# A gated cross-attention and FFN kernel: FFN weights prepared in attention's last iterations, and a new placing of work over the slots of a batch

## The reference

```python
x = x + tanh(g_xattn[0]) * xattn(layernorm(x), ctx, ctx, Wq, bq, Wk, bk, Wv, bv, Wo, bo)
x = x + tanh(g_ffn[0])   * ffn(layernorm(x), w_gate, w_up, w_down)
# xattn: 32 batches, 256 positions, width 256, 16 heads of 16, rotary q and k,
#        keys within 50 positions of the query only, softmax, output projection
# ffn:   every weight is rounded in blocks of 32 to 4 bits and scaled back (lpbq_dequant);
def lpbq_dequant(w):
    wb = w.reshape(O, I // 32, 32)
    s = maximum(max(abs(wb), -1) / 7, 1e-12)
    return (clip(round(wb / s), -8, 7) * s).reshape(O, I)
#        activations are rounded to 16 bits by the largest absolute value of the whole tensor
#        (after x, up, gate, silu(gate), silu(gate) * up), inner width 768
```

## Time and profile before

| | us |
|---|---|
| median of 3 runs | 1405.16 (1403.41 to 1405.55) |
| the profiled execution | 1403.11 |
| its span in the trace | 1401.4 |
| `prepare`, to DVE's first instruction of attention | 48.3 |
| attention, from there to DVE's first instruction of the FFN | 48.3 to 843.0 |
| FFN | 843.0 to the end |

### The profile page before, as it was taken

How to read it: one execution, slowest core, us unless ns; L and a number is a source line. 1 busy time by engine, 2 the same in 40 slices (tenths; PEclk the granted TensorE clock), 3 DMA queues, 4 the chain that set the end, 5 groups by cost and what they waited for, 6 DMA issues and landing times. The chain is left out here.

```text
span 1401.4 us, 27833 instructions
## 1 busy us (share of the span) xinstructions
PE 1209.1 (86%) x8960; PEld 796.4 (57%) x8992; DVE 1214.9 (87%) x3602; ACT 832.9 (59%) x1336; POOL 562.6 (40%) x1360
## 2 busy tenths in 40 slices
PE   3367989898989898998989858999899979977998
PEld 2245666666666666666767643444333334436887
DVE  4678998998998999999999836998899989997986
ACT  2225665666675666667565545664677779983332
POOL 1127777776777777778777640000000000000000
PEclk7679999999999999999999988999999999998999
DMA  3175767666666667675756311222455455556764
GB/s 113 30 166 124 165 140 156 141 156 147 149 149 147 151 146 160 147 160 142 179 128 156 89 35 56 101 103 100 157 186 189 165 180 198 187 177 203 235 237 165
DMA packets 132369, 207.27 MB, mean 148 GB/s; under 512 B 11159, under 2 KB 97050, under 8 KB 126106
## 3 DMA queue, kind: packets, MB, share of 16 engines
q1 hardware_dynamic: 132250, 205.86, 54.0%
HBM read 125.60 MB, written 79.69 MB: 146 GB/s over the span
## 5 line engine op out<-in xcount | busy, mean ns | idle before, releaser
L586 ACT ACTIVATE probs<-psum 128x356 f32<-128x356 f32 x512 | 210.2, 464 | 235.2 <-PE psum L851 235.0
L697 DVE CUSTOM_DVE_ANT_0 psum<-psum,band 128x178 f32<-128x178 f32 x1024 | 318.2, 372 | 18.5 <-PE psum L834 13.0
L519 POOL TENSOR_SCALAR_AFFINE_SELECT probs<-probs 128x154 f32<-128x154 f32 (+1 forms) x512 | 222.9, 444 | 168.0 <-ACT probs L586 163.3
L1013 PE MATMUL psum<-xnT,w_upT 128*128 (+1 forms) x1152 | 260.9, 384 | 19.1 <-DVE maxima L1237 8.8
L1013 PEld LDWEIGHTS psum<-xnT,w_upT 128*128 128x128 f16 x1152 | 109.8, 99 | 170.1 <-issue 32.4
L834 PE MATMUL psum<-k_stack,q_stack 96*128 96x178 bf16 x1024 | 145.7, 246 | 56.2 <-DVE smax L697 50.9
L528 POOL TENSOR_SCALAR_AFFINE_SELECT probs<-probs 128x254 f32<-128x254 f32 (+1 forms) x512 | 189.7, 394 | 0.0
L851 PE MATMUL psum<-q_stack,k_stack 98*128 98x178 bf16 x1024 | 129.5, 242 | 16.1 <-DMA q_stack<-shiftT 9.2
L834 PEld LDWEIGHTS psum<-k_stack,q_stack 96*128 96x128 bf16 x1024 | 75.1, 99 | 119.0 <-DVE smax L697 101.9
L697 DVE DVE_READ_ACCUMULATOR2_ANT smax<- 128x1 f32 x1024 | 142.6, 139 | 0.0
L1613 PE MATMUL psum<-w_downT,xnT 128*128 128x256 f16 x1152 | 128.1, 275 | 16.0 <-DVE xnT L1563 16.0
(11 more groups left out here) (189 smaller groups left out, 2271.1 us busy)
## 6 DMA issues: line engine op xcount, KB each, us to landing
k_parts_scratch<-k_parts SPq DMA_DIRECT2D x32, 384.0 KB, 2.6
q_parts_scratch<-q_parts SPq DMA_DIRECT2D x32, 384.0 KB, 2.6
k_stack<-k_parts_scratch SPq DMA_DIRECT2D x32, 384.0 KB, 5.1
q_stack<-q_parts_scratch SPq DMA_DIRECT2D x32, 384.0 KB, 7.4
gate_scratch<-g_stage SPq DMA_DIRECT2D x16, 768.0 KB, 3.3
g_in<-gate_scratch SPq DMA_DIRECT2D x16, 768.0 KB, 4.6
sig_scratch<-w_gateT SPq DMA_DIRECT2D x32, 384.0 KB, 2.3
sig_again<-sig_scratch SPq DMA_DIRECT2D x32, 384.0 KB, 3.4
```

Of the source, the lines that this page charges most:

```text
L519: nc.gpsimd.affine_select(out=t[:, :, 0:n], in_=t[:, :, 0:n], pattern=[[0, 2], [1, n]], compare_op=ALU.is_ge, fill=0.0, base=WINDOW - off, ...
L586: nc.scalar.activation(ring_tile(probs, b, pair, c)[:].rearrange("p e j -> p (e j)"), scoreT_bank[c][:, 0:2 * SPAN], ACT.Exp, scale=DK ** ...
L697: ins = nc.vector.tensor_tensor_reduce(out=mine, in0=mine, in1=keep["band"][:, t, :], scale=1.0, scalar=-3e38, op0=ALU.add, op1=ALU.max, a ...
L1013: last = nc.tensor.matmul(bank[:], weights[wp][:, c * I + f * P:c * I + (f + 1) * P], x_parts[:, c, bass.ds(j * (2 * TILE) + xp * TILE, TI ...
```

## The change

`prepare` no longer loads or prepares the FFN weights, and has no `partition_all_reduce`. It loads c and x of batch 0 first, then the attention weights in the order Wo, Wk, Wq, Wv, and makes the output bias right after Wo.

The FFN weights are loaded by SP at the beginning of iteration 33 into the buffers of `q_stack` and `k_stack` that are free by then, and prepared in iterations 33 to 35, at slots given by four tables. The largest scale over the partitions is found for `w_gate` and `w_up` per partition, and for `w_down` with a transpose and a small matmul on PE and a reduction on DVE.

In every iteration some work has a new slot. On DVE: `statistics(nxt)` from slot 4 to slot 7; the statistics of `residual` from slot 0 to slot 1; `divide(b3, 0)` from slot 2 to slot 1; the `xmax` reduction from slot 7 of `b4` to slot 1 of `b5`. On POOL the two `scale_of` go from slots 5 and 1 to slots 7 and 2. On ACT the normalising of x goes from slot 7 of the iteration before to slot 0. On PE the x transposes go behind the K projection, the V projection from slot 5 to slot 4, `out_rows(b3, 0)` from slot 1 to slot 0.

```diff
 # prepare, SP
+            sp.dma_start(keep["c_in"][:], rows_c[0]).then_inc(keep["c_loaded"], 16)
+            sp.dma_start(keep["x_in"][:], rows_x[0]).then_inc(keep["x_loaded"], 16)
-            for n in ffn[:1] + attn + ffn[1:]:
+            for n in attn:
...
 # attention
+        nat = {n: t[:].rearrange("p h t -> p (h t)").bitcast(F32)[:, 0:WCOLS]
+               for n, t in zip(ffn, (q_stack[2], k_stack[2], q_stack[0]))}
+        wround = parts["q"][:].rearrange("p k t -> p (k t)").bitcast(I16)
+        SIZE_AT = {(B + 1, 3): 0, (B + 2, 0): 1, (B + 2, 6): 2}
+        ROUND_AT = {(B + 1, 5): 0, (B + 2, 2): 1, (B + 3, 0): 2}
+        SCALE_AT = {(B + 1, 7): 0, (B + 2, 4): 1, (B + 3, 2): 2}
+        TURN_AT = {(B + 2, 1): 0, (B + 2, 3): 1, (B + 2, 5): 2, (B + 2, 7): 3, (B + 3, 1): 4, (B + 3, 3): 5,
+                   (B + 3, 5): 6, (B + 3, 6): 7, (B + 3, 7): 8}
...
+            def load_weights():
+                for n, last in zip(ffn, (B - 3, B - 3, B - 2)):
+                    sp.wait_ge(scoredT, (last + 1) * 2 * PAIRS)
+                    sp.dma_start(nat[n].rearrange("p (o i) -> p o i", o=w[n].shape[0] // P),
+                                 w[n].rearrange("(o p) i -> p o i", p=P)).then_inc(nat_in[n], 16)
             def steps(rnd, unit):
+                if rnd * NBUF + unit == B + 1:
+                    load_weights()
                 load_x(Batch(rnd, unit, -1))
...
 # DVE: size_weight = reduce per block, scale, its largest, reciprocal; round_weight; scale_weight;
 # weight_rest = the low part of one group of four blocks
+                    if at in SIZE_AT:
+                        size_weight(SIZE_AT[at])
+                    if at in ROUND_AT:
+                        round_weight(ROUND_AT[at])
+                    if at in SCALE_AT:
+                        scale_weight(SCALE_AT[at])
+                    if at in TURN_AT:
+                        weight_rest(TURN_AT[at])
+                    if slot == 1:
+                        statistics2(b4)
+                        divide(b3, 0)
+                    if slot == 1 and b5.real:
+                        reached(dve, xn2T_copied, b5, 1, 1)
+                        nc.vector.tensor_reduce(keep["xmax"][:, b5.n:b5.n + 1], ...)
...
 # PE
+            def turn_weight(group):
+                n, _, blks = blocks_of(group)
+                pe.wait_ge(weight_scaled, group // GROUPS + 1)
+                if group < 2:
+                    pe.wait_ge(exp_done, B * 2 * PAIRS)
+                else:
+                    pe.wait_ge(weight_low, group - 1)
...
                         project_dims(bank_b, cT, keep["WkT"]).then_inc(projected["k"], 1)
-                    if slot == 1:
-                        out_rows(b3, 0)
+                        reached(pe, x_normed, b0, T, T)
+                        transpose4(bank_a, xn[:].rearrange("p t d -> p (t d)")).then_inc(x_transposed, 1)
+                    if slot == 4 and b0.real:
+                        reached(pe, multiplied["k"], b0, 4, 4)
+                        project_rows(bank_b, cT, keep["WvT"], False).then_inc(projected["v"], 1)
...
                     scoresT(Batch(rnd, unit, late), pair)
+                    if slot == 0:
+                        out_rows(b3, 0)
```

More of the change, by code:

```diff
@@ L160, in prepare @@
         for n in attn:
[L161 to L170, removed]
+            plan.append([(n, o, c) for c in range(C) for o in range(T)])
         @block.vector
@@ L180, in _ @@
             nc.vector.tensor_copy(keep["identb"][:], keep["ident"][:]).then_inc(ones_set, 1)
[L181 to L221, removed]
@@ L222, in _ @@
[L222 removed]
+            dve.wait_ge(ones_set, 7)
         @block.gpsimd
         def _(pool):
[L226 to L233, removed]
+            for m, (src, dst) in enumerate(((brow, brest), (brest, brest2))):
+                pool.wait_ge(part_step, 2 * m + 1)
+                nc.gpsimd.tensor_tensor(dst[:], src[:], bpart[:, m, :], ALU.subtract).then_inc(part_step, 1)
@@ L599, in shift_copy, with weight_top @@
                                      scale=-1.0).then_inc(shiftT_copied, 1)
+            def weight_top(group):
+                act.wait_ge(weight_transposed, group + 1)
+                nc.scalar.activation(place(group)[0], weight_bank(group)[:], ACT.Copy).then_inc(weight_high, 1)
             def copy_outT(b, half):
@@ L638, in steps @@
                                  attT_copied, [(att_projected, b3.before(1), 1, 1)])
-                        if nxt.real:
-                            normalise(nxt, x_in, xn, scale, scale_ready, x_normed)
                     pair, late = pair_at(slot, ST_FIRST)
                     exps(Batch(rnd, unit, late), pair)
+                    if slot == 0 and b0.real:
+                        normalise(b0, x_in, xn, scale, scale_ready, x_normed)
                     if slot == 4 and b4.real:
@@ L709, in shift_parts, with weight_rest @@
+            def weight_rest(group):
+                top, rest_of = place(group)
+                dve.wait_ge(weight_high, group + 1)
+                nc.vector.tensor_tensor(rest_of, weight_bank(group)[:], top, ALU.subtract).then_inc(weight_low, 1)
             def shift_parts(b, half):
@@ L752, in steps @@
             def steps(rnd, unit):
-                nxt, b0, b1, b2, b3, b4 = (Batch(rnd, unit, k) for k in range(-1, 5))
+                nxt, b0, b1, b2, b3, b4, b5 = (Batch(rnd, unit, k) for k in range(-1, 6))
                 for slot in range(SLOTS):
@@ L774, in steps @@
                         shift_parts(b1, 0)
+                        if nxt.real:
+                            reached(dve, x_loaded, nxt, 16, 16)
+                            statistics(nxt, x_in, stats, moments, stats_taken, moments_taken)
                     pair, late = pair_at(slot, S_FIRST)
@@ L925, in steps @@
                         transpose4(bank_b, xn2[:].rearrange("p t d -> p (t d)")).then_inc(x2_transposed, 1)
-                    if slot == 5 and b0.real:
-                        reached(pe, multiplied["k"], b0, 4, 4)
-                        project_rows(bank_b, cT, keep["WvT"], False).then_inc(projected["v"], 1)
                     if slot == 5:
@@ L974, in steps @@
                             weigh(Batch(rnd, unit, late), pair, b2)
+                    at = (rnd * NBUF + unit, slot)
+                    if at == (B + 2, 7):
+                        turn_largest()
+                    if at in TURN_AT:
+                        turn_weight(TURN_AT[at])
+                    if at == (B + 3, 1):
+                        spread_largest()
             run(steps)
```

193 lines of the change are left out of this document (123 added, 70 removed).

## The result

The changed kernel takes 1368.83 us (median of 3 runs, 1365.31 to 1369.25) against 1405.16. The ratio is 0.9737, its 95% interval 0.9709 to 0.9765. The profiled execution has a span of 1367.1 us against 1401.4, 34.3 us less. Four landmarks on DVE divide the span: its first rope of K, the rope of the fifth batch (from which on the iterations are regular), that of the last batch, and the FFN's first reduction.

What follows compares the result with a forecast made beforehand. It took `prepare` and attention's end as chains of waits and the middle as bound by DVE, PE closely coupled. -31 - 20 + 13 = -38 on 1403.1 gave 1365, so 1367 for the median; range 1348 to 1388.

Steps and rivals of the forecast that it cites:

- the likeliest case: Whole kernel: 1367 us for the median, its own range 1356 to 1378, 52 in 100.
- The beginning: `prepare` and attention's first iteration: attention starts 23.8 us earlier, first rope gains 7.5 more; together 31.3, bounds 24 and 34.
- The steady part: The 31 steady iterations: 15 us from hidden waits plus 5 from fewer half-clock waits, -20; bounds 0 and -35.
- The wait of 0.78: DVE's rope waiting for the K projection in each steady iteration: hidden by the new order with 1.4 us to spare.
- rival 1: Steady iterations: ACT's chain or late rows of maxima take over, period stays at 23.0; 1387 us, 17 in 100.
- The expected wait of 0.2 at `residual`: Steady iterations: ACT's last work delays the output projection to 21.9 us, so DVE waits about 0.2 at `residual`.
- The port term: Steady iterations: `remainder` of k overlaps POOL's q rotation, takes about 1.1 us, 0.1 more; bounds 0.69 and 1.58.
- rival 4: Steady iterations: `remainder` of k takes 1.58 us beside POOL's rotation, q's likewise; iterations lengthen; 1415 us, 4 in 100.
- half of 9.9 us: Steady iterations: half of DVE's waits at `residual` for half-clock output projections goes, 5 us.
- The end: Iterations 33 to 35: late rows +2, DVE weight work +6.8, last stretch to the FFN +4; 13 us, bounds 4 and 26.
- rival 3: End of attention: weight work isn't hidden, moved between exposed places, +26 in place of +13; 1380 us, 7 in 100.
- Rival 2: Steady iterations: K wait and all half-clock projections disappear, and the end costs 9; 1348 us, 20 in 100.

Runs made afterwards that it cites:

- e4: The weight half alone: new `prepare` and weights in iterations 33 to 35, every other operation in its slot from the kernel before; 1382.98 us.
- e5: The slot half alone: the kernel before, with weights still in `prepare`, given the new slots; 1386.43 us.
- e1: The changed kernel with the second layer norm's statistics moved back from slot 1 to slot 0 on DVE; 1349.16 us.
- e2: The changed kernel with `scale_of` of the second layer norm moved back from slot 2 to slot 1 on POOL; 1369.00 us.
- e8: The changed kernel with e7's load order and DVE's weight work moved behind `divide` and the second statistics in iterations 34 and 35; 1361.31 us.
- e7: The changed kernel with `w_up` and `w_down` loaded behind the rows of maxima in iteration 33; 1369.10 us.
- e3: The changed kernel with both edits of e1 and e2: statistics back in slot 0, `scale_of` back in slot 1; 1363.42 us.
- e6: e3 with DVE's cast `shift_parts(b2, 1)` moved behind the rope of q in slot 3; 1360.08 us.

## Why the prediction was right, and where a term was wrong

Predicted 1367, measured 1368.83; the likeliest case came true, and the sum of -38 stands against -34.3 in the profiled span. The terms are less good than the sum.

*The beginning*, -31 predicted, -35.4 measured. The mechanism was right. The size was off in the end of `prepare`: DVE began attention at 20.73, not 24.5. The bias product was done about 1 us sooner than I put it, and POOL's subtraction, for which I had taken the longer of two durations, took the shorter, with less time around it on ACT; from SP's first issue to DVE's start it took 5.5 us, not 6.4. Within attention 7.8 us were gained where 7.5 were worked out. Either half of the change alone gives 4.9 of them (48.34 to 63.07 before, 21.01 to 30.83 in e4, 49.80 to 59.68 in e5), so the two overlap.

*The steady part*, -20 predicted, -10.6 measured. Here a step failed: "The wait of 0.78 is hidden with 1.4 us to spare" is true, but I followed only what the moved work would cover and not what it had covered. The second statistics had stood behind `residual` just where PE, after the output projection, isn't yet at the scores of slot 0. Taken away from there they uncover 1.00 us. A regular iteration has 1.19 us of idle time on DVE before and 1.18 after (the gaps between 394.57 and 417.01, and between 465.38 and 487.86): the wait changed its place. For the regular iteration this is rival 1 in its result, by another cause than the two that rival 1 named: PE's waits for the rows of maxima grew only from 5.8 us in 8 to 9.0 in 10, and those for ACT's copy before the output projection are 1.6 in 4. e1 shows the cause: the statistics back in slot 0, and the wait goes, with 20 us. The 0.64 us of period is a net figure. The wait (1.00) and `remainder` of k (0.72) together lost 1.7; some 1.1 came back, as the wait of 0.19 and in many small steps of DVE.

The expected wait of 0.2 at `residual` didn't come; DVE, held up at the scores, arrives there later than the projection.

The port term had the right mechanism and was too small. I gave `remainder` of k 1.1 us at an overlap of 0.55; the rotation of q ended 1.0 after its start and the operation took about 1.56, near the upper bound (the median of 28 is 1.565, where it was 0.91). That is rival 4's price for k, though not for q, which got shorter (0.89 to about 0.79). By itself it costs little: e2 took the 0.74 us away and the period fell by 0.1, since PE set the pace.

What was gained in the 27 iterations is the spread. Before, five of the 27 iterations took over 24 us (24.1 to 24.8) and the rest 22.2 to 23.1; after, the longest takes 23.4, because `residual` hardly ever waits for an output projection at half clock. By windows of one microsecond the granted clock is at half speed in six stretches between 110 and 720 before (from 127, 230, 322, 346, 438 and 711) and in none after. I had given this half of 9.9 us; nearly all of it went. What exactly keeps the clock up in the new order wasn't tested on its own; e4, with the old slots, has iterations of 24.4, 24.1 and 24.4 us with half-speed stretches at each; with the new ones e5 has one of 24.3 and e8 one of 24.2. That points to the slots, from one profiled execution of each; how much of the 10.6 us is luck of that execution isn't shown.

*The end*, +13 predicted, +10.8 measured. By stretches of DVE, after less before: up to the `residual` of batch 30 +2 predicted, +0.7 measured; to that of batch 31 +6.8 predicted, 21.8 - 15.3 = +6.5 measured; from there to the FFN +4 predicted, +3.6 measured. The first of these was mis-sized: PE did wait 1.49 us for the rows of maxima, but e5, without any weight work, needs the same 53.3 us up to that `residual`, and e7 took the wait away and didn't come there sooner. In the second, the `divide` came 4.8 us later (4.4 predicted) and the rest took 1.7 longer (2.4 predicted). That weight work stood ahead of `divide` was the cause given, and e8 supports it: with it behind, 4.2 of the 4.8 us are back.

What the prediction left out is the clock in this stretch. The last output projection ran at half speed before and after, so the 2.4 us that this costs, with the transposes ahead of it, cancel in the difference; between the experiments they don't. Against e5 the end is 14.0 us longer, and 3.2 us seem to be given back by the new slots, but of both figures 2.4 us are the half clock around this projection. The end's 2.2 us in e7 and 2.4 of the 6.7 in e8 are the same. Whether the new orders keep the clock up or it was so in the one execution that was profiled stays open. In iteration 35 e8 gained nothing, which points to the amount of work there.

The rivals: rival 3 (all of it exposed, 26 us) is refuted by e5: 14.0 us at most are exposed, not 26. Rival 4 (a longer iteration) didn't come: the period fell from 22.93 to 22.54. Rival 2 is refuted for this kernel, and its 1348 is what e1 gives by another road.

## What to carry to other kernels

When an operation is moved to fill a wait, ask what it had been covering where it stood: look at what DVE would meet next there and when that is ready. Two engines that hand work to each other in a fixed order form a loop, and only the work inside the part that the loop runs through counts; shortening an operation elsewhere, or in the part that the other engine covers, turns into a wait. Work that is moved from an idle beginning into an idle end can be hidden only if it stands behind the operations that others wait for. And where one profile of a kernel is set against one of another, look at the granted clock of the stretch before putting a difference down to the edit: here half clock around one projection was worth 2.4 us, as much as an edit seemed to gain.

## What the runs showed of the hardware

A DVE cast of 16 columns can take 1.02 us in place of 0.17 while POOL adds two SBUF tensors, and a DVE subtraction of 512 columns that began while POOL rotated ended 0.55 us after the rotation in each of three rows (406.92 to 407.47 and 429.94 to 430.50 in the earlier trace rows, 478.57 to 479.12 in the changed kernel). POOL's `affine_select` did not hold DVE up in that way: in the regular iteration above, the cut behind the rotation was stretched, to 1.14 us for two where 0.69 to 0.77 is usual. DVE's subtraction had begun 0.98 us ahead of that cut; which of the two yields when the cut is first isn't shown. The Trainium skill (SBUF — State Buffer, section Who interferes with whom) lists casts among the operations that can contend with GpSimd, when their operands meet its conditions, and the traces of e3 and e6 agree for this small one: 1.02 against 0.27 us.

Before the change POOL idled 5.94, 6.76 and 5.77 us with nothing to wait for when it went from its additions to `partition_all_reduce` and back; without the reductions in `prepare` these times are gone, and one of 5.59 stays ahead of the reduction at attention's end. The Trainium skill (GPSIMD Engine Reference, section 2.1 Instruction dispatch) gives about 6 us for loading the code at the first call to a freshly loaded kernel. The idle times are of that size, but the three in `prepare` stand at changes between the two operations in both directions, behind earlier calls of each, which the rule for a first call alone doesn't say.
